# Adding an attention mask on TensorE and reading scores straight from PSUM in a fused graph kernel

## The reference

```python
qkv = h @ W
qkv = qkv.reshape(Bn, Nn, 3, H, HEAD_DIM).transpose(2, 0, 3, 1, 4)
q, k, v = (qkv[0], qkv[1], qkv[2])
mask = jnp.where(adj == 0, -jnp.inf, 0.0)
scores = jnp.einsum('bhid,bhjd->bhij', q, k) / np.sqrt(HEAD_DIM) + mask
attn = jax.nn.softmax(scores, axis=-1)
out = jnp.einsum('bhij,bhjd->bhid', attn, v)
```

## Time and profile before

| | |
|---|---|
| median of 3 runs | 1528.53 us (1525.26 to 1529.06) |
| the profiled execution | 1526.68 us |
| its span, first to last instruction | 1524.9 us |
| mean granted TensorE clock over the span | 0.889 of full |
| layers, the four trips | from about 712 us to the end |
| DMA | 8 GB/s on average |

### The profile page before, as it was taken

How to read it: one execution, slowest core, us unless ns; L and a number is a source line. 1 busy time by engine, 2 the same in 40 slices (tenths; PEclk the granted TensorE clock), 3 DMA queues, 4 the chain that set the end, 5 groups by cost and what they waited for, 6 DMA issues and landing times.

```text
span 1524.9 us, 27023 instructions
## 1 busy us (share of the span) xinstructions
PE 1066.0 (70%) x6001; PEld 843.0 (55%) x6001; DVE 1170.7 (77%) x5634; ACT 800.8 (53%) x2905; POOL 177.6 (12%) x464
## 2 busy tenths in 40 slices
PE   5777777777763000003998878997889988899885
PEld 4555555555542000002687666895657966678764
DVE  6888888888889988995556685467874577845677
ACT  3444444444421000000676776777867778667776
POOL 2111111111120000000111101012020110201111
PEclk9999999999996555555999989998999998999997
DMA  0000000000030000000000001000010000100000
GB/s 2 0 0 0 0 0 0 0 0 0 0 74 0 1 1 1 1 1 28 28 1 2 1 9 51 1 1 1 1 58 1 1 1 2 29 1 1 1 1 28
DMA packets 19857, 12.50 MB, mean 8 GB/s; under 512 B 1153, under 2 KB 18722, under 8 KB 19746
## 3 DMA queue, kind: packets, MB, share of 16 engines
q1 hardware_dynamic: 19746, 11.23, 2.8%
HBM read 7.03 MB, written 4.19 MB: 7 GB/s over the span
## 4 chain that ended last, share of the span: by engine, by line
PE 31%; DVE 11%; ACT 8%; issue 2%; POOL 1%; DMA 0%; DVEq 0%; POOLq 0%; ACTq 0%
PE P L1038 11%; PE P L983 6%; PE P L1046 5%; PE P L988 2%; ACT x L1140 2%; ACT S L1211 2%; DVE stats L1250 2%; PE P L1100 1%; DVE S L1322 1%; DVE top L1327 1%; DVE t L1340 1%; PE P L1055 1%; PE P L1084 1%; POOL t L971 1%; ACT t L1191 1%
## 5 line engine op out<-in xcount | busy, mean ns | idle before, releaser
L195 PE MATMUL productP<-M,tail_ident 128*128 128x128 f32 x254 | 100.8, 500 | 72.8 <-DVE M L315 72.8
L463 PE MATMUL sumP<-tail_ident,Yb 128*128 128x128 f32 x1 | 0.5, 476 | 215.8 <-DVE Yb L625 215.8
L1038 PE MATMUL P<-t,WihT 128*128 128x128 f32 (+1 forms) x832 | 119.3, 290 | 9.8 <-POOL t L971 9.8
L195 PEld LDWEIGHTS productP<-M,tail_ident 128*128 128x128 f32 x254 | 63.6, 311 | 110.5 <-DVE M L315 110.5
L1046 PE MATMUL P<-step_h,WhhT 128*128 128x128 f32 (+2 forms) x768 | 123.4, 304 | 0.0
L492 ACT ACTIVATE small<-small 128x1 f32<-128x1 f32 x1 | 0.2, 203 | 227.5 <-DVE small L598 227.5
L463 PEld LDWEIGHTS sumP<-tail_ident,Yb 128*128 128x128 f32 x1 | 0.2, 183 | 215.9 <-DVE Yb L625 215.9
L1038 PEld LDWEIGHTS P<-t,WihT 128*128 128x128 f32 x832 | 109.9, 191 | 13.3 <-POOL t L971 12.6
L964 POOL TENSOR_TENSOR rstd<-variance,minus_half 128x4 f32<-128x4 f32 x64 | 64.5, 1008 | 445.1 <-DVE variance L1260 445.1
L1163 ACT ACTIVATE gate_i<-P,half_bias 128x128 f32<-128x128 f32 (+3 forms) x160 | 69.2, 433 | 87.8 <-PE P L1046 65.0
L1046 PEld LDWEIGHTS P<-step_h,WhhT 128*128 128x128 f32 x768 | 108.9, 191 | 4.5 <-DVE step_h L1293 0.7
(11 more groups left out here) (322 smaller groups left out, 3142.6 us busy)
## 6 DMA issues: line engine op xcount, KB each, us to landing
xin<-x SPq DMA_DIRECT2D x16, 256.0 KB, 2.8
out<-y SPq DMA_DIRECT2D x16, 256.0 KB, 2.3
W<-L_gnn_W SPq DMA_DIRECT2D x3, 64.0 KB
Wqkv<-L_gnn_W SPq DMA_DIRECT2D x1, 192.0 KB
Wg<-L_gnn_Wg SPq DMA_DIRECT2D x2, 64.0 KB
A<-adj SPq DMA_DIRECT2D x1, 64.0 KB, 1.8
b<-L_gnn_b SPq DMA_DIRECT2D x1, 64.0 KB
bg<-L_gnn_bg SPq DMA_DIRECT2D x1, 64.0 KB
```

Source lines behind the costliest of these rows:

```text
L195: pe.matmul(productP[:, 0:N], tails, M[:], start=True, stop=True).then_inc(product_ready, 1)
L1038: last = pe.matmul(place, c["WihT"][:, p - 1, gate * H:(gate + 1) * H], sources(s, p, t), start=bank not in fresh, stop=not t, skip_group_ ...
```

## The change

PE writes the mask into each of the two banks first, as a matmul of the identity with the mask (repeated for the four graphs), which opens the accumulation; the 8 score matmuls then add to it. The one for bank 1 stands ahead of the wait for v_copied (first pair) or mixed_copied (second pair), the one for bank 0 behind it. The scale of the scores goes into the copy of the queries. VectorE takes the negated maximum of each bank straight from PSUM, with a signal for each head, and no longer writes S. ScalarE takes the exponentials from PSUM into S, and waits for the maxima head by head.

```diff
--- before.py
+++ after.py
@@ -925,7 +925,7 @@
                s, trip)
 
         def on_pair(name, r, s, trip):
-            what = {"masked": "scores", "tops": "scores", "tops_ready": "scores", "scores_ready": "scores",
+            what = {"masked": "scores", "tops": "scores", "tops_ready_0": "scores", "tops_ready_1": "scores", "scores_ready": "scores",
                     "probs_ready": "softmax", "mixed_ready": "mixed", "mixed_copied": "mixed"}.get(name, "probs_turned")
             at(name, [(what, n) for n in range(HEADS // PAIR)], r, s, trip)
 
@@ -1089,16 +1089,21 @@
                 elif name[0] == "scores":
 
                     r = name[1]
+                    masks = c["mask"][:, None, :].to_broadcast([N, G, N])
                     if r == 0:
                         on("k_copied", s, trip)
+                        pe.matmul(P[s][1][:], ident, masks, start=True, stop=False, skip_group_check=True)
                         on("v_copied", s, trip)
                     else:
+                        pe.matmul(P[s][1][:], ident, masks, start=True, stop=False, skip_group_check=True)
                         on_pair("mixed_copied", r - 1, s, trip)
+                    pe.matmul(P[s][0][:], ident, masks, start=True, stop=False, skip_group_check=True)
                     for b in range(G):
                         for h in range(PAIR):
                             at = (r * PAIR + h) * HEAD
                             last = pe.matmul(P[s][h][:, b * N:(b + 1) * N], qT[s][at:at + HEAD, b, :],
-                                             kT[s][at:at + HEAD, b, :], start=True, stop=True, tile_position=(at, 0))
+                                             kT[s][at:at + HEAD, b, :], start=False, stop=True, tile_position=(at, 0),
+                                             skip_group_check=True)
                     last.then_inc(S_("scores_ready"), 1)
                 elif name[0] == "probs_turned":
                     on_pair("probs_ready", name[1], s, trip)
@@ -1199,17 +1204,17 @@
                     copy(flat(xT, s), P[s][1][:], "x3T_copied", s)
                 elif name == "qkv":
                     on("q_ready", s, trip)
-                    copy(flat(qT, s), P[s][0][:], "q_copied", s)
+                    A_.activation(flat(qT, s), P[s][0][:], ACT.Identity, scale=float(HEAD) ** -0.5).then_inc(S_("q_copied"), 1)
                 elif name == "values":
                     on("v_ready", s, trip)
                     copy(flat(wh, s), P[s][0][:], "v_copied", s)
                 elif name[0] == "softmax":
-                    on_pair("tops_ready", name[1], s, trip)
                     for h in range(PAIR):
+                        on_pair(f"tops_ready_{h}", name[1], s, trip)
                         for b in range(G):
                             k = h * G + b
-                            last = A_.activation(S[s][:, h, b, :], S[s][:, h, b, :], ACT.Exp, bias=ntop[s][:, k:k + 1],
-                                                 accum_out=total[s][:, k:k + 1])
+                            last = A_.activation(S[s][:, h, b, :], P[s][h][:, b * N:(b + 1) * N], ACT.Exp,
+                                                 bias=ntop[s][:, k:k + 1], accum_out=total[s][:, k:k + 1])
                     last.then_inc(S_("probs_ready"), 1)
                 elif name[0] == "probs_turned":
                     on_pair("probs_turned_a", name[1], s, trip)
@@ -1319,14 +1324,8 @@
                     r = name[1]
                     on_pair("scores_ready", r, s, trip)
                     for h in range(PAIR):
-                        last = V.scalar_tensor_tensor(S[s][:, h], P[s][h][:].rearrange("n (g m) -> n g m", g=G),
-                                                      float(HEAD) ** -0.5, c["mask"][:, None, :].to_broadcast([N, G, N]),
-                                                      ALU.mult, ALU.add)
-                    signal(last, "masked", s)
-                    on_pair("masked", r, s, trip)
-                    signal(V.reduce_max(top[s][:], S[s][:].rearrange("n h g m -> n (h g) m"), AX_X), "tops", s)
-                    on_pair("tops", r, s, trip)
-                    signal(V.tensor_scalar(ntop[s][:], top[s][:], -1.0, None, ALU.mult), "tops_ready", s)
+                        signal(V.tensor_reduce(ntop[s][:, h * G:(h + 1) * G], P[s][h][:].rearrange("n (g m) -> n g m", g=G), AX_X, ALU.max,
+                                               negate=True), f"tops_ready_{h}", s)
                 elif name[0] == "probs_turned":
                     r = name[1]
                     on_pair("probs_ready", r, s, trip)
```

## The result

The changed kernel takes 1555.75 us (median of 4, 1553.43 to 1558.11), the one before 1527.67 in the same comparison: a ratio of 1.0185 with a 95% interval of 1.0172 to 1.0198. It is slower by 28 us, where 1551 was forecast with a range of 1541 to 1561. Its profiled execution took 1553.43 us with a span of 1551.7, 26.8 more than the span before.

The account below looks back on a forecast made before the run. PE was taken to bound the stretch's first part, VectorE its second; PE's queue with masks added 5.4 us per trip and 6.1 in the last, together 22.2, giving 1551 us, range 1541 to 1561.

Parts of the forecast that it names:

- the stretch: In each trip, first score matmul to VectorE's first L1344, 866.99 to 903.12 in trip 1; forecast to end 5.4 us later.
- VectorE's part: Per scores stage, 2.65 us of mask and maximum work replaced by 1.33 of reductions; 42 us saved over 32 stages if VectorE-bound.
- Rival 4: VectorE's reduction with negation as dear as mask and maximum together; time would hardly move; counted with the forecast's 0.84.
- ScalarE's part: Softmax exponentials read from PSUM: eight take 2.72 us against 3.08; starting on the first reduction is worth nothing.
- PE's part: Two mask matmuls per scores stage at 0.86 us each: 1.72 per stage, 13.8 per trip, 55 over 32 stages.
- The walk: Sum along PE's queue, first scores to slot 0's heads_turned: 40.70 us plus 0.75 wait; L1344 at 908.5, +5.4 per trip.
- The wait for the two softmaxes: PE at probs_turned of slot 0's second pair waits some 0.75 us for ScalarE's softmaxes of slots 3 and 0.
- The rule weighed: Slot 3's first and slot 0's second scores, masks between: 2.18 us, not 1.65, as weights load under matmuls only across differing row groups.
- VectorE as the bound throughout: Rival 1: masks hide in PE's idle time and 42 us are gained, 1486; chance 0.04.
- Cheap mask streams: Rival 2: masks cost 0.51 us per 512 columns like L988's transposes, so not slower, 1529; chance 0.07.
- the point given for them: Break-even for the masks in PE's queue without waits: 1.15 us per stage, 0.57 per mask, from 9.2 us per trip.
- Dearer scores: Rival 3: accumulating onto the mask ends the overlap of two heads' scores, +28 us, 1579; chance 0.05.

## Why the prediction was right, point by point

**What bounds the kernel.** Right. PE was full in the first part of the stretch and had room in the second; the two runs with masks for one pair show it directly, +17 us against +1.4. The 77% of VectorE in the earlier trace rows said nothing of it.

**VectorE's part.** A pair of reductions takes 1.29 us and 1.33 had been taken; 42 us less busy time were foreseen and measured. That their worth is small is borne out, too: all the relief together with free masks gives 18 us. Rival 4, a reduction as dear as mask and maximum together, is refuted.

**ScalarE's part.** 0.34 us per exponential, as worked out from the earlier trace rows. The signal by head was held to be worth nothing, and is.

**PE's part.** 0.86 us per mask was right for the first of a stage (866.35 to 867.21). The second steps by 0.95 (867.21 to 868.16), 0.09 more, at the change to the scores with their weights of 32 rows, 0.7 per trip; the lower bound had even allowed for a gain there. This 0.09 isn't new, it has moved: before, the turn and probs_turned stood ahead of the scores and carried it, and ahead of a mask they are shorter than taken, the turn 0.44 for 0.53 (865.91 to 866.35), probs_turned 0.93 for 1.02 (891.72 to 892.65). That gives back 0.6 per trip, so that only 0.1 to 0.2 is left of this term. A mask right behind scores steps by 0.97 (887.71 to 888.68), and the values ahead of mixed by 1.09 for 0.99 (881.79 to 882.88), 0.2 more together.

**The walk.** 41.5 us were forecast from PE's first mask to L1343, 42.77 measured. The wait for the two softmaxes is where it was expected, at the probs_turned of slot 0's second pair, and there is no other. Its size was 1.01 us for 0.75, and the prediction's own two times, 898.54 and 897.9, make only 0.64. PE waiting more than 1 us in all had been named as a sign of being wrong; 1.01 is just past that mark, though the wait is the one that was foreseen. What the walk missed is the step at its end: I had let VectorE take the heads as soon as PE had turned them, which in the trace of the changed kernel would be 907.79 + 0.66 = 908.45, but ahead of them in VectorE's queue stand the reductions of slot 3's second scores, 907.91 to 909.1, and that is another 0.6 us per trip. In the kernel before, too, L1344 starts right behind slot 3's scores and not behind the turned heads:

```profile
900.48 1.28 DVE L1322 SCALAR_TENSOR_TENSOR S<-P,mask 128x512 f32<-128x512 f32 x2
901.79 1.22 DVE L1327 TENSOR_REDUCE top<-S 128x8 f32<-128x1024 f32 x1
903.04 0.17 DVE L1329 TENSOR_SCALAR ntop<-top 128x8 f32<-128x8 f32 x1
```

Together the terms make +6.6 per trip for 5.4, and +7.4 in the last for 6.1; 27.2 for 22.2. That 6.6 lies under the upper bound of 7.1 is in part luck: the bound came from exponentials at 3.08 us and 0.13 more per stage, the exponentials came at 8 x 0.34 as taken, and the step that was missed stood in no bound.

**From L1343 on** VectorE runs without gaps and unchanged, 15.87 us to the next trip's first bias in both traces, so nothing is given back. This had been named as a way to be wrong.

**The rule weighed.** Slot 3's first scores and slot 0's second ones step by 1.09 each behind their own masks (886.62 to 887.71, and 889.63 to 890.72), 2.18 and not 1.65 for the two. Without masks, in the trace of that run, they adjoin again and take 1.65 (1079.16 to 1080.81). The rule of the Trainium skill (TensorE: Matmul & The Clock Gate, Part 3, What overlaps and what doesn't) agrees with both, but it doesn't hold for all weights here. The timelines of PE and of its weight loads in the changed kernel:

```profile
871.11 1.02 PE L1085 MATMUL P<-xT,Wqkv 128*128 128x512 f32 x2
...
871.54 0.14 PEld L988 LDWEIGHTS P<-tail_ident,x 128*128 128x128 f32 x1 [0.24 <-issue]
...
873.26 0.19 PEld L1100 LDWEIGHTS P<-mask,tail_ident 128*128 128x128 f32 x1 [0.24 <-issue]
874.21 0.97 PEld L1104 LDWEIGHTS P<-kT,qT 32*128 32x128 f32 x16 [0.76 <-issue]
```

The first scores' weights are loaded only at 874.21, behind the mask's stream, as the rule has it, and that is where the 0.09 stands. But the turn's weights, which have all 128 rows like L1085's, are loaded at 871.54, while L1085 runs from 871.11 to 872.13; with "only" where the row groups differ the rule would exclude that. There the trace decides.

**The rivals.** VectorE as the bound throughout is refuted by the run without masks (1509, not 1486). Cheap mask streams are refuted for float32 by the trace, and the point given for them, even at 1.15 us per stage, is close: one mask at 0.96 us per stage gives +0.2%. Dearer scores are refuted: 16 records step by 1.09, as before, also when they accumulate.

## What to carry to other kernels

Before work is moved from the busiest engine to the next one, find the stretch that it is in and read there whose queue has gaps: 32 mask matmuls cost 17 us where PE's queue was full and 1.4 where it waited for the engine being relieved. If a matmul only adds constants that bfloat16 holds, give it bfloat16 operands: the same masks then cost 0.53 us per stage instead of 1.81, and the change turns from 1.9% slower to 0.4% faster, to about 1% with one copy moved off the engine that is late next. In a walk along one queue, end it with what stands ahead of the last taker in the taker's own queue. A step taken from one neighbour belongs to the pair: when something is put between two instructions, read both steps anew.

## What the runs showed of the hardware

A bfloat16 matmul with 512 columns into a float32 accumulation has one record and steps by 0.22 us, a float32 one has two records and steps by 0.86. A float32 matmul with 512 columns and full-width weights, followed by one with weights of 32 rows, steps by 0.95 instead, and the bfloat16 one by 0.31, in both cases some 0.09 more; the 32-row weights are then loaded only behind the stream (874.21), while weights of 128 rows are loaded under it (871.54). VectorE takes a negated maximum over 512 columns of PSUM in the time of the two-input operation on 512 columns of PSUM, 1.29 us for two in either. The granted clock differed between executions of one kernel in a stretch that starts with the same gaps of 1.25 and 1.5 us (0.96 and 0.86), and that trip came out 3.4 us longer. In one execution of the bfloat16 kernel it differed between trips: behind the same wait of 1.70 us it stayed at 1.00 in trips 1 and 3, and the stretch had 0.95 and 0.91 in trips 2 and 4, 1.5 and 3.0 us longer.
